# Rebuilding the opening and the last projected quarter of a fused attention, normalisation and expert kernel, and placing its tiles at round addresses

## The chip, the core and the metric

The kernel runs on one core of one Trainium2 chip. The metric is the device time of one execution in microseconds. Six engines matter in the text: TensorE with its weight loads (PE, PEld), VectorE (DVE), ScalarE (ACT), GpSimd (POOL) and SyncE (SP), which issues most DMAs. Each engine plays one list of instructions in order and waits on semaphores.

## What is computed

The reference has 4 sequences of 512 tokens of width 512. Each is projected to keys and values, a test-time recurrence runs over 32 mini-batches of 16 tokens for 16 heads of width 32, and its output is normalised, projected, added to the input and normalised again. Then 8 experts (two for each token) and one shared feed-forward work on the tokens, and a last normalisation follows.

```python
k, v = x @ Wk.T, x @ Wv.T                      # heads of width 32; rotary on k
def step(W, kv):                               # 32 of these, one after the other
    kc, vc = kv
    z = einsum('bhsd,bhde->bhse', kc, W)
    grad = einsum('bhsd,bhse->bhde', kc, (z - vc) * inv_n)
    return W - LR * grad, z
x = layernorm(x + (layernorm(z) * gamma + beta) @ Wo.T)
routed = sum over the two best experts of (silu(x Wg) * (x Wu)) Wd
x = layernorm(x + routed + shared(x))
```

## The kernel before

Every large product is done in three matmuls on float32r pieces: a tile is split into a high part (an ACT copy, for instance `xh`, `GH`, `XH`, `OH`) and a low part (a subtraction on DVE or POOL, `xl`, `GL`, `XL`, `OL`), and high times high, high times low and low times high are added up in one bank.

The 2048 tokens are worked on in four quarters of 512 (8 steps of the recurrence each). The first quarter's keys and values are projected ahead of the recurrence (`first`), behind `WARM` small matmuls that run while the first data are still on their way. Then the list `for n in range(LAST + 1)` builds 72 slots by hand. Slot n = 2s holds `scan_z` and `scan_r` of step s (PE, then a subtraction on DVE and four masked copies on ACT), slot 2s + 1 holds `scan_g` (PE) and the copies of the state W (ACT). Behind these, `slot(n)` places other work: the out-projection of a block of 128 tokens in `STAGES` (`t_one`, `t_wo_`, `t_three`, `router` on PE; `zt`, `stats_one`, `stats_two`, `norm_two`, `residual`, `out_rows` on the others), and half units of the projection of the next quarter (`products`, 6 matmuls of 512 columns; `HALVES` says how many in each of the 16 slots of a quarter). A quarter has 8 units of two halves: even units are keys (stationary `WH[:, 0]`, which shares its memory with the gate weights `GH[:, 0]`), odd ones values. `arrange` takes a unit out of its bank; a key passes through the rotary step over three slots (ACT, POOL, DVE shuffle, POOL, DVE add, DVE transpose), whose later parts wait in the list `later`.

In the opening, `wo_scale`, `wo_gamma`, `wo_sum`, `wo_bias`, `wo_means`, `wo_centre`, `wo_high` and `wo_low` make the out-projection's weights: its rows are scaled by gamma, the mean over rows is taken off, and the result is split into `OH` and `OL`. The first user is `t_wo_(0)` in slot 7.

From slot 48 on no quarter is left to project. There the generator `shared_01` hands out the shared expert in pieces: a quarter of a gate and up product (`gate_up_steps`, eight pieces of 6 matmuls for a weight block w and a token quarter q) or a quarter of a down product (`down_steps`). `FILL` gives each slot a budget; a piece costs 1.3. The tokens that these products read come from `turn_x(i)`: four transposes into a bank, then `XH` on ACT and `XL` on DVE; quarters 0 and 2 go to `XH0`, 1 and 3 to `XH1`. Bank 6 is also used by `t_one` and `router`, bank 7 by `t_wo_` and `t_three`; banks 4 and 5 by projections and by the first pieces of the shared expert. Behind slot 71 come the rest of the shared blocks 0 to 3, the routing, 23 expert strips (`gate_up_r` with 256 columns, `gate_up_s` with one strip of 128 tokens, `down_r`), the other shared blocks, and the sums.

Tiles are placed one behind the other in the order in which they are declared, small ones taking a multiple of 32 bytes. Added up, `xh`, `xl`, `GH`, `GL`, `ah`, `XH0` and `XL0` start at a multiple of 128 bytes, `XH1`, `XL1`, `RH`, `RL`, `OH`, `OL` and `oh`, `ol` 32 bytes behind one.

Of the kernel before, what the change touches and what calls it, by code (L numbers as in the profile page):

```python
# [12 lines left out]
NT = 16  # L13
# [9 lines left out]

HALVES = (2, 1, 2, 0, 2, 1, 1, 0, 2, 1, 1, 0, 2, 1, 0, 0)


WARM = 14
# [51 lines left out]
def program(nc, xT, xtok, wkT, wvT, woT, gam, bet, wg, wgu, wd, wsgu, wsd, cosd, sind, maskd, negid, identd, lowd, constd, upd, out):  # L79
    ctx = ExitStack()  # L80
    with ctx:
# [9 lines left out]

        x1 = sb(ctx, "x1", [NT, 512])
        ident = sb(ctx, "ident", [128])
# [8 lines left out]
        logits = sb(ctx, "logits", [NT, 8])  # L102
        comb = sb(ctx, "comb", [NT, 8])
        low = sb(ctx, "low", [8, 8])
        mhalf = sb(ctx, "mhalf", [1])
        st = sb(ctx, "st", [4, 6])
        mv = sb(ctx, "mv", [4, 2])
        rstd = sb(ctx, "rstd", [4, 2])
# [9 lines left out]
        eid = ctx.enter_context(nc.sbuf_tensor("eid", [128, RT], mybir.dt.int32))  # L118
# [64 lines left out]
        def split_g(w, ks=(0, 2)):  # L183
            p = w % 2
            f = (gused[w - 2],) if w >= 2 else (a_last[w],)
            out = gdone_.get(w, ())
            for k in ks:
                out += split(GH[:, p, k:k + 2, :], GL[:, p, k:k + 2, :], graw[:, rawp(w), k:k + 2, :], gloaded[w], free=f, rest=PO if w < 2 else DV)
            gdone_[w] = out
# [14 lines left out]
        def high_g0(k):  # L204
            return AC.op(lambda e: e.activation(GH[:, 0, k:k + 2, :], xr[:, k:k + 2, :], ACT.Copy), gloaded[0], a_last[0])

# [25 lines left out]
        mask = part(pa, "late", "mask", [64])  # L232
# [3 lines left out]
        W = [part(pa, "late", "WA", [256]), part(pa, "late", "WB", [256])]  # L236
        colsum = part(pa, "late", "colsum", [512])
        onesr = part(pa, "late", "onesr", [128], F32R)
# [3 lines left out]
        x1f = part(pa, "late", "x1f", [4, 128])  # L242
        wgs = part(pa, "late", "wgs", [4, 8])

# [27 lines left out]
        red = part(ctx, "first", "red", [3, NT])  # L272
        ce = sb(ctx, "ce", [4, 2, 8])
# [9 lines left out]

        ah = sb(ctx, "ah", [2, 2, 512], F32R)
# [76 lines left out]
        def wo_sum(key, src, tok, at):  # L361

            a = PO.op(lambda e: e.tensor_tensor(sums[:, at, :], src[:, 0, :], src[:, 1, :], ALU.add), tok[0], tok[1])
            b = PO.op(lambda e: e.tensor_tensor(sums[:, at + 1, :], src[:, 2, :], src[:, 3, :], ALU.add), tok[2], tok[3])
            t_sum[key] = PO.op(lambda e: e.tensor_tensor(sums[:, at, :], sums[:, at, :], sums[:, at + 1, :], ALU.add), a, b)
# [989 lines left out]
```

How the kernel before makes its waits and increments, by code:

```python
    def play(self, eng):  # L62
        for it in self.items:
            if it[0] == "w":
                eng.wait_ge(it[1], it[2])
            else:
                ins = it[1](eng)
                if it[2] is not None:
                    ins.then_inc(it[2], it[3])
```

## Time and profile before

| | us |
|---|---|
| median of 3 runs | 742.47 (741.02 to 742.95) |
| the profiled execution | 742.71 |
| its span, first to last instruction | 740.9 |
| PE busy in the span | 712.2 (96%) |
| DVE, ACT, POOL busy | 451.5, 343.7, 344.2 |

PE is the engine to look at: the chain of work that ended last lies on PE for 88% of the span. A busy PE still hides two kinds of time, matmuls that follow one another at a wider pitch, and stretches in which the clock that is granted to it is at the lower of its two levels. Pitch is read from the start times of neighbouring rows, the clock from the table of stretches.

### The profile page before, as it was taken

The numbers are of one execution on the slowest core, as the hardware profiler recorded it, in microseconds if no ns is written. First come the engines' busy times: TensorE is split into PE (matmuls) and PEld (weight loads), VectorE is DVE, ScalarE is ACT, GpSimd is POOL, SyncE is SP. The second block draws the span as 40 slices with busy tenths as digits, with TensorE's granted clock in tenths as the row PEclk, the third lists the DMA queues.
The fourth block names the chain that finished last, engine by engine and source line by source line (L and its number), as shares of the span: only waits on it lengthen the run. The fifth ranks groups of instructions, "written<-read, shape, count | busy, mean of one in ns | idle before, by whom it ended". The sixth has DMA issues, their size and how long they took to land.

```text
span 740.9 us, 17740 instructions
## 1 busy us (share of the span) xinstructions
PE 712.2 (96%) x7472; PEld 597.1 (81%) x7472; DVE 451.5 (61%) x753; ACT 343.7 (46%) x663; POOL 344.2 (46%) x361
## 2 busy tenths in 40 slices
PE   9997999999979998999999999999999999999994
PEld 8665788888867777778888898999989978888883
DVE  3755574575554455358883876676666627777554
ACT  5542454453444544242112576777767733241232
POOL 2784665566554644001102375565655335536332
PEclk9998999999999999999999999999999999999998
DMA  8120121112023213000402389999999875424221
GB/s 272 70 74 2 60 86 33 31 62 85 31 74 100 88 60 130 0 28 1 170 1 58 123 270 339 319 328 288 318 326 326 290 229 162 124 84 114 72 86 71
DMA packets 53263, 99.71 MB, mean 135 GB/s; under 512 B 5120, under 2 KB 14080, under 8 KB 53184
## 3 DMA queue, kind: packets, MB, share of 16 engines
q1 hardware_dynamic: 47504, 79.96, 32.0%
q0 software_dynamic: 5680, 18.62, 8.2%
q8 instruction: 59, 0.97, 0.5%
q14 instruction: 20, 0.16, 0.1%
HBM read 79.95 MB, written 18.61 MB: 133 GB/s over the span
## 4 chain that ended last, share of the span: by engine, by line
PE 88%; DVE 5%; ACT 2%; POOL 2%; DMA 1%; issue 1%; SPq 0%; POOLq 0%; DVEq 0%; ACTq 0%
PE bank L693 23%; PE bank L717 11%; PE bank L401 11%; PE bank L1120 11%; PE bank L608 7%; PE bank L1168 6%; PE bank L532 4%; PE bank L507 4%; PE bank L1137 3%; PE bank L1095 2%; PE bank L640 2%; DMA RAW<-in_wsgu 1%; PE bank L577 1%; PE bank L655 1%; PE bank L304 1%
## 5 line engine op out<-in xcount | busy, mean ns | idle before, releaser
L199 POOL TENSOR_TENSOR xl<-RAW,xh 128x1024 fp32r<-128x1024 f32 x31 | 75.1, 2422 | 122.6 <-ACT xh L198 95.1
L214 ACT ACTIVATE ah<-sg 128x512 fp32r<-128x512 f32 (+1 forms) x64 | 33.6, 525 | 158.4 <-DVE sg L669 149.2
L693 PE MATMUL bank<-XH,GH 128*128 128x512 f32 x256 | 103.1, 403 | 4.0 <-DVE XL L215 2.5
L693 PE MATMUL bank<-XL,GH 128*128 128x512 f32 x256 | 101.0, 395 | 0.0
L693 PE MATMUL bank<-XH,GL 128*128 128x512 f32 x256 | 101.0, 394 | 0.0
L215 DVE TENSOR_TENSOR GL<-RAW,GH 128x1024 fp32r<-128x1024 f32 (+2 forms) x63 | 81.1, 1325 | 10.8 <-ACT GH L214 9.7
L550 POOL TENSOR_SCALAR rstd<-mv 128x1 f32<-128x1 f32 x48 | 14.4, 300 | 142.9 <-DVE mv L549 142.2
L1056 POOL DMA_INDIRECT xg<-x1d,idxu x39 | 49.8, 1276 | 61.6 <-DVE idxu L1037 40.4
L518 DVE TENSOR_TENSOR r<-bank,vst 128x256 f32<-128x256 f32 x64 | 26.4, 422 | 84.0 <-PE bank L507 83.3
L1120 PE MATMUL bank<-RH,GH 128*128 128x256 f32 x256 | 72.9, 285 | 0.0
L1120 PE MATMUL bank<-RH,GL 128*128 128x256 f32 x256 | 71.5, 279 | 0.0
L1120 PE MATMUL bank<-RL,GH 128*128 128x256 f32 x256 | 71.5, 279 | 0.0
L214 ACT ACTIVATE GH<-RAW 128x1024 fp32r<-128x1024 f32 (+2 forms) x69 | 65.4, 996 | 1.8 <-DMA RAW<-in_wsgu 1.2
L669 DVE TENSOR_TENSOR sg<-sg,bank 128x512 f32<-128x512 f32 (+1 forms) x64 | 35.0, 547 | 51.2 <-PE bank L693 30.3
L521 ACT ACTIVATE r<-r,mask 128x128 f32<-128x128 f32 x128 | 41.0, 391 | 43.7 <-DVE r L518 43.7
L693 PEld LDWEIGHTS bank<-XH,GH 128*128 128x128 f32 x256 | 48.4, 189 | 15.5 <-ACT oh L582 2.2
L215 DVE TENSOR_TENSOR al<-sg,ah 128x512 fp32r<-128x512 f32 (+1 forms) x64 | 37.3, 583 | 37.8 <-ACT ah L214 37.1
L693 PEld LDWEIGHTS bank<-XH,GL 128*128 128x128 f32 x256 | 48.5, 189 | 11.2
L693 PEld LDWEIGHTS bank<-XL,GH 128*128 128x128 f32 x256 | 48.5, 190 | 10.2
L401 PE MATMUL bank<-xh,GH 128*128 128x512 f32 x128 | 53.4, 418 | 0.0
L401 PE MATMUL bank<-xl,GH 128*128 128x512 f32 x128 | 50.5, 394 | 1.4 <-POOL xl L747 1.4
L717 PE MATMUL bank<-xh,ah 128*128 128x512 f32 x128 | 51.0, 398 | 0.4 <-ACT sg L667 0.3
(218 smaller groups left out, 1765.5 us busy)
## 6 DMA issues: line engine op xcount, KB each, us to landing
RAW<-in_wgu SPq DMA_DIRECT2D x23, 1024.0 KB
RAW<-in_wd SPq DMA_DIRECT2D x23, 512.0 KB
yd<-RAW SPq DMA_DIRECT2D x39, 256.0 KB
RAW<-in_wsgu SPq DMA_DIRECT2D x14, 512.0 KB
x<-in_xtok SPq DMA_DIRECT2D x16, 256.0 KB, 3.8
x1d<-x SPq DMA_DIRECT2D x16, 256.0 KB, 2.1
RAW<-in_wsd SPq DMA_DIRECT2D x8, 512.0 KB
out_x<-x SPq DMA_DIRECT2D x16, 256.0 KB, 2.0
```

Of the source, the lines that this page charges most:

```text
L199: b = PO.op(lambda e: e.tensor_tensor(DL[:, p, :, :], draw[:, rawp(w), :, :], DH[:, p, :, :].bitcast(F32), ALU.subtract), a, dloaded[w], *f)
L214: a = AC.op(lambda e: e.activation(hi, src, ACT.Copy), *tokens, *free)
L215: b = rest.op(lambda e: e.tensor_tensor(lo, src, hi.bitcast(F32), ALU.subtract), a, *tokens, *free)
L401: t = PE.op(lambda e, k=k, wt=wt, xx=xx, n=n: e.matmul(bank[b][:], wt[:, j, k, hg * 128:hg * 128 + 128], xx[:, k, :], start=(k == 0 and n ...
L521: rtok[h] = AC.op(lambda e, b=b: e.activation(r4[:, :, b, :], r4[:, :, b, :], ACT.Copy, scale=mask[:, 32 * b:32 * b + 1]), s, t_c2)
L608: t = PE.op(lambda e, k=k, aa=aa, ww=ww, n=n: e.matmul(bank[b][:], aa[:, k, :], ww[:, k, :], start=(n == 1), stop=(n == 12)), state["oh"], ...
L669: m = DV.op(lambda e: e.tensor_tensor(sg[:, w, 0:cols], sg[:, w, 0:cols], bank[bu][:, 0:cols], ALU.mult), a, tu)
L693: t = PE.op(lambda e, b=b, k=k, c=c, wt=wt, xx=xx, n=n: e.matmul(bank[b][:], wt[:, p, k, c:c + 128], xx[h][:, k, :], start=(n == 1), stop= ...
L717: t = PE.op(lambda e, b=b, k=k, j=j, aa=aa, ww=ww, n=n: e.matmul(bank[b][:], aa[:, ap, k, j * 128:j * 128 + 128], ww[:, p, k, :], start=(n ...
L1056: PO.items.append(("i", lambda e, h=h: e.indirect_dma_start(xg[:, j % 2, h, :], None, x1d, bass.IndirectOffsetOnAxis(ap=idxu[:, first + h: ...
L1120: t = PE.op(lambda e, b=b, k=k, c=c, wt=wt, xx=xx, n=n: e.matmul(bank[b][:, 0:256], wt[:, pw, k, c:c + 128], xx[:, p, k, :], start=(n == 1 ...
L1168: t = PE.op(lambda e, b=b, k=k, h=h, aa=aa, ww=ww, n=n: e.matmul(bank[b][:], aa[:, p, k, h * 128:h * 128 + 128], ww[:, pw, k, :], start=(n ...
```

## The change

- Opening: 10 warm-up matmuls in place of 14. The transposes `a4` and `a6` of two key units leave the place ahead of the value units and go into `later`, so that they stand behind the first `scan_r`. Quarter 1's halves are handed out by a list of their own, `OPENING`. Of the four low parts of quarter 1's input, two stay on POOL and two go to DVE, by way of `later`; the three additions for the mean of the weights go from POOL to DVE, also by `later`. `wo_bias` moves from slot 1, bank 7, to slot 2, bank 6, behind `wo_means`.
- Last projected quarter: `UNITS` projects the key units 0, 2, 4 and 6 in places 0, 1, 2 and 4. The gate weights of the first shared block are split in slots 41 and 42 (before: 45 and 46), the turn-ins of tokens go to slots 44 (two), 45 and 46, in banks 6 and 7 (before: slots 46 and 47, banks 4 and 5), and the table load for Silu to slot 36 (before: 41).
- Shared expert: the budget begins in slot 47, `down_steps(1, 0)` is put ahead of `gate_up_steps(0, 1)`, and block 1's gate split goes to slots 51 and 52 with its low part on DVE (before: 52 and 53, POOL).
- Homes: declarations are put in another order with three fillers, so that every large tile starts at a multiple of 1024 bytes.

The diff, cut to its core:

```diff
+UNITS = (0, 2, 4, 1, 6, 3, 5, 7)
 HALVES = (2, 1, 2, 0, 2, 1, 1, 0, 2, 1, 1, 0, 2, 1, 0, 0)
-WARM = 14
+OPENING = (1, 1, 0, 1, 2, 1, 2, 0, 2, 1, 2, 0, 2, 1, 0, 0)
+WARM = 10
...
+        sb(ctx, "padh", [88])
         x1 = sb(ctx, "x1", [NT, 512])
...
+        part(pa, "late", "padl", [288])
...
+        sb(ctx, "padf", [136])
         ah = sb(ctx, "ah", [2, 2, 512], F32R)
...
+        def high_g1(k):
+            return AC.op(lambda e: e.activation(GH[:, 1, k:k + 2, :], graw[:, 0, k:k + 2, :], ACT.Copy), gloaded[1], a_last[1])
+
+        def low_g1(k, a):
+            b = DV.op(lambda e: e.tensor_tensor(GL[:, 1, k:k + 2, :], graw[:, 0, k:k + 2, :], GH[:, 1, k:k + 2, :].bitcast(F32), ALU.subtract),
+                      a, gloaded[1], a_last[1])
...
-        def wo_sum(key, src, tok, at):
+        def wo_sum(key, src, tok, at, Q):
...
-            t = PE.op(lambda e: e.matmul(bank[7][:], onesr[:].bitcast(F32), sums[:, 0, :], start=True, stop=True),
-                      t_ones, t_sum["bias"], *free[7])
+            t = PE.op(lambda e: e.matmul(bank[6][:], onesr[:].bitcast(F32), sums[:, 0, :], start=True, stop=True),
+                      t_ones, t_sum["bias"], *free[6])
...
         first(1, [3])
-        a4()
-        a6()
...
-            b = (PO if q == 1 else DV).op(lambda e: e.tensor_tensor(xl[:, k, :], xr[:, k, :], xh[:, k, :].bitcast(F32), ALU.subtract), a, tok, last_unit[0])
-            xs[q, k] = (a, b)
+            def rest():
+                b = (PO if q == 1 and k < 2 else DV).op(...)
+                xs[q, k] = (a, b)
+            if q == 1 and k >= 2:
+                later.append(rest)
+            else:
+                rest()
...
-            if n == 47:
-                turn_x(2)
-                turn_x(1)
+            if n == 44:
+                turn_x(0, base=6)
+                turn_x(1, base=6)
...
-            if n in (46, 47):
-                turn_x(3 * (n - 46))
-            if n == 41:
+            if n == 45:
+                turn_x(3, base=6)
+            if n == 46:
+                turn_x(2, base=6)
+            if n == 36:
                 AC.op(lambda e: e.activation(rstd[:, 3, 0:1], mhalf[:], ACT.Silu), t_mh)
             if q + 1 < NB:
-                for _ in range(HALVES[loc]):
+                for _ in range((HALVES if q else OPENING)[loc]):
...
-            if n == 1:
-                wo_bias()
             if n == 2:
                 wo_means()
+                wo_bias()
...
-            if n in (45, 46):
-                g0 = high_g0(2 * (n - 45))
-                later.append(lambda: low_g0(2 * (n - 45), g0))
+            if n in (41, 42):
+                g0 = high_g0(2 * (n - 41))
+                later.append(lambda: low_g0(2 * (n - 41), g0))
...
-            if n in (52, 53):
-                split_g(1, (2 * (n - 52),))
+            if n in (51, 52):
+                g1 = high_g1(2 * (n - 51))
+                later.append(lambda: low_g1(2 * (n - 51), g1))
...
             yield from down_steps(0, 0)
+            yield from down_steps(1, 0)
             yield from gate_up_steps(0, 1)
-            yield from down_steps(1, 0)
...
-        FILL = {n: SCAN[n % 4] for n in range(48, 64)}
+        FILL = {n: SCAN[n % 4] for n in range(47, 64)}
...
+        later.extend([a4, a6])
         for k in range(4):
             split_x(1, k, xraw[1])
-        wo_sum("bias", wob, t_wob, 0)
-        wo_sum("mean", wor, t_wosc, 2)
+        wo_sum("bias", wob, t_wob, 0, PO)
+        later.append(lambda: wo_sum("mean", wor, t_wosc, 2, DV))
```

## Rows read from the trace of the kernel before

**Rows 1.** The waits of PE: who waited for whom, us in total, times, longest

```profile
PE bank L608 <- DVE OL L387: 4.0, 1, 4.0
...
PE bank L693 <- DVE XL L215: 2.5, 2, 2.0
...
PE bank L693 <- ACT sg L667: 1.3, 1, 1.3
...
PE bank L608 <- DVE ol L587: 1.0, 1, 1.0
```

**Rows 2.** Table of stretches: length, PE busy (instructions), granted clock, DMA share, GB/s

```profile
62.00:68.60 6.60, 5.76 (x28) 0.50 0.01 2
...
294.00:297.30 3.30, 3.30 (x8) 0.50 0.31 119
435.00:585.00 150.00, 150.00 (x1033) 1.00 0.94 315
```

**Rows 3.** Timeline of PE, opening: start, length, line, tiles, count

```profile
1.45 6.14 PE L304 MATMUL bank<-colsum 128*128 128x128 f32 x28 [1.45 <-DVE colsum L300]
...
30.20 0.65 PE L507 MATMUL bank<-WA,RAW 32*32 32x64 f32 x32
...
44.98 1.02 PE L375 MATMUL bank<-RAW,onesr 128*128 128x512 f32 x2
...
68.22 0.85 PE L507 MATMUL bank<-WA,RAW 32*32 32x64 f32 x32
```

**Rows 4.** Timeline of PE in an undisturbed quarter: starts of slots 24 to 28

```profile
127.73 0.65 PE L507 MATMUL bank<-WA,RAW 32*32 32x64 f32 x32
...
131.70 1.10 PE L532 MATMUL bank<-r,RAW 32*32 32x64 f32 x64
...
134.69 0.65 PE L507 MATMUL bank<-WA,RAW 32*32 32x64 f32 x32
...
137.69 1.10 PE L532 MATMUL bank<-r,RAW 32*32 32x64 f32 x64
...
142.43 0.65 PE L507 MATMUL bank<-WA,RAW 32*32 32x64 f32 x32
```

**Rows 5.** Timeline of DVE in the opening

```profile
29.36 1.29 DVE L442 STREAM_TRANSPOSE RAW<-RAW 128x512 f32<-128x512 f32 x2
30.58 2.46 DVE L447 STREAM_TRANSPOSE vst<-bank 128x512 f32<-128x512 f32 x4
33.17 0.75 DVE L518 TENSOR_TENSOR r<-bank,vst 128x256 f32<-128x256 f32 x2
...
53.67 2.82 DVE L387 TENSOR_TENSOR OL<-x,OH 128x512 fp32r<-128x512 f32 x2
```

**Rows 6.** Timeline, PE and DVE, slots 44 to 47

```profile
202.45 0.87 DVE L518 TENSOR_TENSOR r<-bank,vst 128x256 f32<-128x256 f32 x2 [3.28 <-PE bank L507]
...
202.76 0.50 PE L401 MATMUL bank<-xh,GH 128*128 128x512 f32 x1
...
203.87 0.71 DVE L613 SCALAR_TENSOR_TENSOR x<-bank,rstd,x 128x512 f32<-128x512 f32 x1
...
209.72 0.66 PE L631 MATMUL bank<-ident,x 128*128 128x128 f32 x4
...
211.78 0.18 DVE L549 BATCH_NORM_AGGREGATE mv<-st 128x2 f32<-128x6 f32 x1
...
215.79 1.94 PE L655 MATMUL bank<-ident,x 128*128 128x128 f32 x8 [3.94 <-DVE XL L215]
```

**Rows 7.** Table of stretches for L693 alone: a product from XH0, one from XH1

```profile
659.50:670.75 11.25, 11.02 (x48) 9.01 (x48) 1.00 0.17 57
...
692.20:703.70 11.50, 11.33 (x48) 8.94 (x48) 1.00 0.06 23
```

**Rows 8.** Timeline of PE: third and last matmul of one 48 of L1120

```profile
486.64 0.28 PE L1120 MATMUL bank<-RH,GL 128*128 128x256 f32 x1
...
491.89 0.28 PE L1120 MATMUL bank<-RH,GL 128*128 128x256 f32 x1
```

More of the change, by code:

```diff
@@ L89, in program @@
         bank = [ctx.enter_context(nc.psum_tensor(f"bank{i}", [128, 512], F32)) for i in range(8)]
+        ident = sb(ctx, "ident", [128])
+        logits = sb(ctx, "logits", [NT, 8])
+        low = sb(ctx, "low", [8, 8])
+        st = sb(ctx, "st", [4, 6])
+        mhalf = sb(ctx, "mhalf", [1])
+        mv = sb(ctx, "mv", [4, 2])
+        rstd = sb(ctx, "rstd", [4, 2])
+        eid = ctx.enter_context(nc.sbuf_tensor("eid", [128, RT], mybir.dt.int32))
+        sb(ctx, "padh", [88])
         x1 = sb(ctx, "x1", [NT, 512])
-        ident = sb(ctx, "ident", [128])
         RAW = sb(ctx, "RAW", [2, 4096])
@@ L187, in split_g @@
             for k in ks:
-                out += split(GH[:, p, k:k + 2, :], GL[:, p, k:k + 2, :], graw[:, rawp(w), k:k + 2, :], gloaded[w], free=f, rest=PO if w < 2 else DV)
+                out += split(GH[:, p, k:k + 2, :], GL[:, p, k:k + 2, :], graw[:, rawp(w), k:k + 2, :], gloaded[w], free=f, rest=DV)
             gdone_[w] = out
@@ L242, in program @@
         x1f = part(pa, "late", "x1f", [4, 128])
+        W = [part(pa, "late", "WA", [256]), part(pa, "late", "WB", [256])]
+        onesr = part(pa, "late", "onesr", [128], F32R)
+        mask = part(pa, "late", "mask", [64])
         wgs = part(pa, "late", "wgs", [4, 8])
+        part(pa, "late", "padl", [288])
         vst0 = sb(pa, "vst0", [8, 256])
@@ L272, in program @@
         red = part(ctx, "first", "red", [3, NT])
+        comb = part(ctx, "first", "comb", [NT, 8])
         ce = sb(ctx, "ce", [4, 2, 8])
@@ L769, in slot @@
                     fn(i)
-            if n in (46, 47):
-                turn_x(3 * (n - 46))
-            if n == 41:
+            if n == 45:
[3 more added lines that the diff above has]
+            if n == 36:
                 AC.op(lambda e: e.activation(rstd[:, 3, 0:1], mhalf[:], ACT.Silu), t_mh)
             if q + 1 < NB:
-                for _ in range(HALVES[loc]):
+                for _ in range((HALVES if q else OPENING)[loc]):
                     halves[0] += 1
-                    u, second = divmod(halves[0] - 1, 2)
-                    u %= 8
-                    last_proj[0] = products(q + 1, u, 4 + u % 2, (2, 3) if second else (0, 1))
+                    at, second = divmod(halves[0] - 1, 2)
+                    at %= 8
+                    u = UNITS[at] if q == 2 else at
+                    last_proj[0] = products(q + 1, u, 4 + at % 2, (2, 3) if second else (0, 1))
                     if second:
                         a_last[u % 2] = last_proj[0]
-                        later.append(arrange(q + 1, u, 4 + u % 2, last_proj[0]))
+                        later.append(arrange(q + 1, u, 4 + at % 2, last_proj[0]))
             if loc >= 14 and q + 2 < NB:
```

26 lines of the change are left out of this document (9 added, 17 removed).

## The prediction, made before the changed kernel ran

> **What bounds the kernel now.** I read the waits of PE first, then the table of stretches with the granted clock, then the timelines of the places that these name. PE is busy for 96% of the span and on the chain that ended last for most of it, so only time that PE loses can be won. It loses it in three ways. First, waits: 4.0 us in slot 7, where the first out-projection waits for the low part of its weights; 3.94 us in slot 47, where a turn-in waits for the XL of the one before it; 2.0 and 0.5 us ahead of first gate products; 1.3 and 1.0 us behind short queues [rows 1, 6]. Secondly, behind the three long ones PE runs at the lower of its two levels (0.50 of 2.4 GHz) for a while: 6.6 us after the first, 3.3 us after the last [rows 2]. Thirdly, the pitch of the big matmuls differs with the operand: 48 of them that stream XH0 take 11.02 us, 48 that stream XH1 take 11.33 us, on the same line at the same clock [rows 7]. In the 150 us of expert strips PE is busy throughout [rows 2], so what is won before them should reach the end.
>
> **The change part by part.** All sums are made against the profiled execution's 742.71 us.
>
> (a) WARM. 28 records of warm-up take 6.14 us, 0.21 us each; four matmuls fewer are 8 records, 1.7 us [rows 3]. But they ran at the lower level, as their pitch tells (four transposes of 128 columns take 0.66 us, tail included, at the upper one [rows 6]), and real matmuls in their place would too until the clock rises. Ends: 0 and 1.7 us. I take the middle, 0.9: at half clock half of the freed time's work gets done.
>
> (b) The opening, slots 0 to 7. Before, PE goes from the first scan_z at 30.20 to that of slot 8 at 68.22, 38.0 us, and does 9 halves [rows 3]. After, I follow DVE, which is the late engine. Its last key add ends near 28.7 (0.75 earlier than before, from (a)). The two key transposes (1.29) are no longer ahead: value transposes 2.46, to 31.2; scan_r's two subtractions 0.75, to 31.9 (before 33.9); then the key transposes, to 33.2, which is when scan_g(0) can run; before, it stood behind 12 matmuls whose low parts POOL made one by one. Then the two xl that DVE now makes: two such subtractions beside a busy POOL took 2.82 us, 1.41 each, against 0.7 for a DVE operation by itself [rows 5, 6], so to 36.05. Three sums follow, one still beside POOL's sums: 1.4 + 0.7 + 0.7, to 38.85. Queued behind them are scan_r(1) and the first rotary step; who waits is wo_means on PE. PE does scan_z(0) at 29.3, one half to 33.2, scan_g(0) to 34.3, the second half as xl comes to 36.5 and scan_z(1) to 37.6, and idles 1.25 us. wo_means and wo_bias take 1.02 each [rows 3], so scan_g(1) starts at 40.9.
>
> From there undisturbed lengths hold [rows 4]: a slot with scan_z and two halves 3.97, one with scan_g, t_one and a half 2.99, one with scan_g, t_wo_ and router 4.74 (0.9 of it router). A half is 6 x 0.23 = 1.38. Slots 3 to 7: 2.5 + 3.97 + 2.99 + 3.97 + 3.84 = 17.3. Is OL ready at 55.5, when t_wo_(0) wants it? On DVE: wo_centre behind the rotary add to 44.9, scan_r(2), a block transpose, wo_centre to 47.6; the first wo_low pair to 49.5; the second stands behind scan_r(3), the block's statistics and a shuffle and ends between 55.7 and 56.5. So 0.6 us of wait, in place of 4.0, and no fall of the clock. Slot 8 starts at 40.9 + 17.3 + 0.6 = 58.8 (58.9 with the rounding of steps), with 8 halves done instead of 9, which costs 1.38 later: 68.22 - 58.9 - 1.38 = 7.9 us, of which (a) is 0.9. **(a) 0.9, (b) 7.0.** Ends of (b): 2 (below) and 9.
>
> On DVE the rows say that a two-input operation beside POOL costs about twice its 0.7 us [rows 5, 6]. The Trainium skill (SBUF — State Buffer, "SBUF: two separate sides") says why: a DVE operation with two SBUF inputs and a GpSimd one hold a shared port pair exclusively, and the later one blocks. By it each of the three sums could wait out a whole POOL operation, which speaks against giving them to DVE; that is the second rival's mechanism. The trace agrees, with 1.41 against 0.7 us.
>
> (c) Turn-ins, slots 44 to 47. Key units first make the rotary table's memory free by slot 42, so XH0 may be written in slot 44. The gate splits (two DVE subtractions, two ACT copies) go to slots 41 to 43, where DVE is idle for 3.28 us ahead of slot 44's scan_r [rows 6] and the two take some 2.5; I cost them at nothing, and if that cover were gone scan_r(44) would come later by what is over. What goes: 3.94 us of idling, and the lower clock behind it (eight transposes in 1.94 us instead of about 1.1 [rows 6], and three matmuls near twice their pitch): 0.8 + 0.5 us. What comes: bank 7 is freed for turn_x(1) by stats_two's DVE operation, which ends at 204.58, while PE would be there 0.5 us after 202.76: 1.3 us. Bank 6 is freed for turn_x(2) by bn_aggr, which ends at 211.96, while t_three ends at 210.2: 1.8 us [rows 6]. 5.2 - 3.1 = **2.1**. Queued behind these waits on PE are two halves and scan_g(47). Ends: 0.4, if the clock falls in the thin stretch of slot 46, and 5.2.
>
> (d) Slots 48 to 63. The XL wait of 0.5 and the Silu wait of 1.3 go [rows 1]. The new budget gives 2, 1, 1, 1 pieces in a group of four slots (2, 1, 2, 0 before); an act_part then falls just ahead of scan_r(50) on DVE and ahead of a second piece in slot 56. No row has that order; nearest are short waits of 0.2 to 0.3 us, ends 0 and 1.3. I take 0.2. **1.6.** Block 1's low gate parts leave POOL for DVE, two operations of the kind of (c) in slots 52 and 53, where DVE waits for PE as in slot 44: nothing, or at most a late scan_r. SP's issues and POOL's down split are not moved; the Silu table load only changes its slot on ACT, which is idle half of the time.
>
> (e) Slots 64 to 71. The turn-ins of quarter 1 are followed by three pieces of down(1, 0), which read nothing new: the 2.0 us wait and the lower clock (8 matmuls at 0.43 instead of 0.23 us: 1.6) go [rows 1, 2], also the 1.0 us for ol, as no act_part is ahead of stats_one(15). New: an act_part in slot 67 stands ahead of stats_two(15), whose result t_three(15) wants three pieces later. No row shows it; ends 0 and 3.9, and I take 1.7, near the queue waits of 1.0 to 2.0 us. **2.9.**
>
> (f) Homes. Of the lines with 512 columns, those whose streamed and stationary tiles start at the same distance from a multiple of 128 bytes run like XH0's; a product from XH1 has its streamed tile 32 bytes off its weights and takes 0.31 us more per 48 [rows 7]. Eight such products: 2.5 us. The strips' L1120 streams RH, 32 bytes off GH, too: 45 intervals in 5.25 us, 116.7 ns [rows 8], about half of XH1's 236. In XH0's proportion it would be 113.5: 768 x 3.2 = 2.5 us. Here DMA is busy 0.94 of the time [rows 2], so I take 2.0. **4.5**; ends 0 and 5.
>
> A rule speaks against (f). The rows show two pitches at one clock, 230 and 236 ns over whole products. The Trainium skill (TensorE: Matmul & The Clock Gate, "Wait — 56ns, not 53.3ns?") gives the warm distance as columns over 2.4 GHz plus 2.5 ns, with no place for an address. By it (f) is nought. The trace doesn't agree: both values lie over its 216.
>
> Sum: 0.9 + 7.0 + 2.1 + 1.6 + 2.9 + 4.5 = 19.0, so 723.7 in an execution like the profiled one, and **723.5** against the median, which lies 0.24 lower.
>
> **The rivals.**
> *Homes do nothing.* The two pitches come from something else about quarters 1 and 3. For it: no row tells how a home could slow a stream. Against it: one line, one weight tile, one clock, and only the streamed tile differs [rows 7]. 723.5 + 4.5 = 728.0.
> *The opening stays late.* Every DVE step beside POOL costs 1.4 to 1.8, OL comes 2.4 us later, t_wo_(0) waits 3.0 us and the clock falls again (2.6). (b) is 2: 728.5. For it: rows 5.
> *The tail's waits only change place.* (c) and (e) are nought: the clock falls in slot 46, and t_three(15) waits long. 728.5.
> *Slower: equal starts collide.* If tiles that start alike hinder each other, all 1578 fast matmuls of 512 columns pay. At XH1's price (6.5 ns) that is 10.3 us against the 14.5 won elsewhere; it decides from 9.2 ns. At twice the price, 13 ns, 742.5 - 14.5 + 20.5 = 748.5. Against it: L401 streams xh against weights that start alike, and is at the narrow pitch.
>
> **How the numbers follow.** Forecast (719 to 727) 0.53, homes 0.13, opening 0.17, tail 0.10, slower 0.02, several together and so within 0.3% 0.02, two together or better than 719 0.03. The range takes in the single rivals and the upper ends of (b) and (c): 715 to 731.5. A measurement tells about 0.3% from no change: faster 0.96, same 0.02, slower 0.02.
>
> **What would show it.** Slot 8's scan_z near 58.9 with a wait for OL under 1 us; no stretch at 0.50 between the warm-up and the end; new waits of L655 on DVE of 1 to 2 us in slots 44 and 46; XH1's 48 in 11.02; L1120 under 115 ns. Wrong it would be if OL is still awaited for 3 us, or if slot 46 runs at the lower level.

## The result and the profile after

| | before | after |
|---|---|---|
| median, us | 742.1 (4 runs, 741.02 to 742.95) | 731.51 (4 runs, 730.34 to 731.92) |
| ratio, 95% interval | | 0.9859 [0.9844, 0.9875] |
| profiled execution, us | 742.71 | 730.34 |
| its span, us | 740.9 | 728.5 |

The changed kernel is 10.6 us faster by the medians and 12.4 by the two profiled executions. 723.5 was forecast, with a range up to 731.5; the measured 731.51 lies just above its upper end. The three executions without a trace lie at 731.49 to 731.92.

The first view is the waits of PE in the changed kernel (who waited for whom, us in total, times, longest), which answers [rows 1].

```profile
PE bank L642 <- ACT x L631: 1.9, 1, 1.9
PE bank L728 <- DVE x L731: 1.8, 2, 1.0
...
PE bank L666 <- DVE mv L560: 1.4, 1, 1.4
PE bank L666 <- DVE x L624: 1.4, 1, 1.4
PE bank L543 <- ACT r L532: 0.9, 3, 0.4
...
PE bank L619 <- DVE OL L400: 0.4, 1, 0.4
```

The 4.0 us for OL are 0.4, the turn-in's 3.9 and the two for XL are gone. In their place stand three waits that were forecast, `t_three(15)` (L642, 1.9) and the two turn-ins (L666), and two that were not: down products (L728) that wait for DVE to empty a bank.

The second view cuts the span into stages. Its rows are from the timeline of PE (start, length, line, tiles) and give the starts of slots 0, 8, 44, 48 and 63, of the first routed product, and of the first and the last gate-up product of the late shared blocks.

```profile
29.68 0.43 PE L518 MATMUL bank<-WA,RAW 32*32 32x64 f32 x16 [0.34 <-DVE RAW L449]
...
59.31 0.41 PE L518 MATMUL bank<-WA,RAW 32*32 32x64 f32 x13
...
194.24 0.36 PE L518 MATMUL bank<-WA,RAW 32*32 32x64 f32 x11
...
214.02 0.37 PE L518 MATMUL bank<-WA,RAW 32*32 32x64 f32 x12
...
274.96 0.42 PE L543 MATMUL bank<-r,RAW 32*32 32x64 f32 x16
...
404.39 0.36 PE L1142 MATMUL bank<-RH,GH 128*128 128x256 f32 x1
...
587.11 0.39 PE L704 MATMUL bank<-XH,GH 128*128 128x512 f32 x1
...
695.91 0.39 PE L704 MATMUL bank<-XH,GH 128*128 128x512 f32 x1
```

The differences of such starts, made in the same way for other kernels of this study, are the lengths of the stages in us. "Work only" is the changed kernel with the addresses of before, "addresses only" the kernel before with the new ones, "mended" comes below.

| stage | before | addresses only | work only | after | mended |
|---|---|---|---|---|---|
| up to slot 0 | 30.20 | 29.18 | 29.34 | 29.68 | 28.80 |
| slots 0 to 7 | 38.02 | 37.74 | 29.54 | 29.63 | 30.08 |
| slots 8 to 43 | 133.52 | 133.57 | 134.73 | 134.93 | 134.95 |
| slots 44 to 47 | 20.57 | 21.73 | 19.83 | 19.78 | 16.70 |
| slots 48 to 62 | 62.99 | 63.08 | 60.81 | 60.94 | 60.94 |
| slot 63 to the first routed product | 132.39 | 131.47 | 130.31 | 129.43 | 126.58 |
| expert strips | 181.48 | 182.72 | 181.41 | 182.72 | 181.48 |
| late shared blocks, to the last gate-up | 109.88 | 108.80 | 109.88 | 108.80 | 108.80 |
| from there to the end | 31.86 | 31.51 | 32.08 | 32.60 | 31.50 |

Two entries are to be corrected before they are read as gains: the opening now does one half less, which comes back in slots 8 to 43 (1.41), and one piece of the shared expert (1.38) has moved from slots 48 to 62 into slots 44 to 47. The stages behind slot 63 show what the addresses do, since work only and before agree there but for the known waits: the expert strips are 1.2 to 1.3 longer with them, the late shared blocks 1.1 shorter.

The third view is the timeline of PE again, for the pitch: first and last matmul of a product of 48 with XH1 in the changed kernel, and the third and the last of a routed product, as in [rows 8].

```profile
630.63 0.39 PE L704 MATMUL bank<-XH,GH 128*128 128x512 f32 x1
...
641.29 0.39 PE L704 MATMUL bank<-XH,GL 128*128 128x512 f32 x1
...
497.35 0.28 PE L1142 MATMUL bank<-RH,GL 128*128 128x256 f32 x1
...
502.75 0.28 PE L1142 MATMUL bank<-RH,GL 128*128 128x256 f32 x1
```

47 intervals in 10.66 us are 226.8 ns, the pitch of XH0, as forecast. 45 intervals in 5.40 us are 120.0 ns where [rows 8] have 116.7: the routed products became slower, not faster. [rows 8] show one of the better ones: over all sixteen such products the mean is 117.2 before and 119.9 after.

### The profile page after: what moved, and what is told of

It reads as the page before. It is cut to its first block, busy times and chain, and to the rows that moved or that the text cites. A ratio compares the mean times of both kernels' runs of the same rounds, so it can differ in the third digit from the quotient of the medians.

```text
span 728.5 us, 17730 instructions
## 1 busy us (share of the span) xinstructions
PE 705.4 (97%) x7464; PEld 593.1 (81%) x7464; DVE 460.9 (63%) x760; ACT 343.0 (47%) x663; POOL 331.6 (46%) x354
## 4 chain that ended last, share of the span: by engine, by line
PE 67%; DVE 14%; POOL 5%; ACT 5%; issue 4%; DMA 3%; SPq 1%; POOLq 0%; DVEq 0%; ACTq 0%
PE bank L704 12%; PE bank L1142 11%; PE bank L414 8%; PE bank L1190 6%; PE bank L619 6%; PE bank L728 5%; PE bank L543 4%; PE bank L518 3%; PE bank L1159 3%; DVE x L731 2%; PE bank L1117 2%; POOL xg L1243 2%; DMA xg<-yd,SI 2%; DVE x L1251 2%; PE bank L651 2%
## 5 line engine op out<-in xcount | busy, mean ns | idle before, releaser
L225 DVE TENSOR_TENSOR GL<-RAW,GH 128x1024 fp32r<-128x1024 f32 (+2 forms) x63 | 83.2, 1359 | 10.0 <-ACT GH L224 8.8
L224 ACT ACTIVATE GH<-RAW 128x1024 fp32r<-128x1024 f32 (+2 forms) x67 | 63.3, 994 | 0.7 <-DMA RAW<-in_wgu 0.3
L728 PE MATMUL bank<-xh,ah 128*128 128x512 f32 x128 | 51.1, 399 | 2.0 <-DVE x L731 1.8
```

The source lines that it names most:

```text
L224: a = AC.op(lambda e: e.activation(hi, src, ACT.Copy), *tokens, *free)
L225: b = rest.op(lambda e: e.tensor_tensor(lo, src, hi.bitcast(F32), ALU.subtract), a, *tokens, *free)
L728: t = PE.op(lambda e, b=b, k=k, j=j, aa=aa, ww=ww, n=n: e.matmul(bank[b][:], aa[:, ap, k, j * 128:j * 128 + 128], ww[:, p, k, :], start=(n ...
```

## The experiments

**Does the sum of addresses come to 4.5 us?** `homes_only` is the kernel before with the new declarations alone, `work_only` the changed kernel without them.

```diff
+        sb(ctx, "padh", [88])
...
+        part(pa, "late", "padl", [288])
...
+        sb(ctx, "padf", [136])
```

> The kernel before with the new tile addresses alone, its order of work untouched. The forecast priced the addresses at 4.5 us (2.5 in the products of XH1, 2.0 in L1120), which gives 737.6. The trace of the changed kernel speaks for another sum: XH1's products there went from 233.4 to 226.7 ns each (2.5 us won), but the routed products of 256 columns went from 117.4 to 120.0 ns (about 2.0 us lost) and their companions of 512 columns from 232.4 to 227 (0.5 won), so 1.0 is left, 741.1; if the last stage is held by VectorE as the changed kernel's trace suggests, only 0.2 of it. If addresses do nothing, 742.1. Decisive in the trace: the pitch of L1120's successor, 120 if the address sets it, 117 if something in the new order does.

Measured: 741.56 against 741.32, ratio 0.9998 [0.9987, 1.0009]. The addresses alone give nothing that can be measured, although XH1's products have the narrow pitch in this trace too. In the table 0.9, 1.1 and 0.35 are won in the three stages with XH1's products and 1.2 are lost in the strips, which leaves 1.1. Another 1.1 are lost in slots 44 to 47, where the lower clock behind the old wait lasted 7 us instead of 3.5; no run shows that the addresses cause that.

> The changed kernel with the addresses of the kernel before: the opening and the last projected quarter alone. The forecast gives 742.5 less 14.5 (0.9 + 7.0 + 2.1 + 1.6 + 2.9), 728.0, and says that it loses 4.5 to the changed kernel. If the addresses are worth 1.0 or less, it stands within 1 us of the changed kernel, at 731 to 732.5. The routed products of 256 columns should then show 117.4 ns again and the late products of XH1 233.4.

Measured: 729.93 (729.73 to 732.31), ratio 0.9856 [0.9836, 0.9877], as fast as the changed kernel with its 0.9859. The two experiments agree: the new addresses as a whole are worth nothing that can be measured, and the 12.4 us are the work's.

**Which address costs?** `rh32` moves RH and RL alone by 32 bytes.

```diff
+        part(ctx, "first", "padr", [8])
         RH = part(ctx, "first", "RH", [2, 4, 256], F32R)
...
-        sb(ctx, "padf", [136])
+        sb(ctx, "padf", [128])
```

> The changed kernel with RH and RL alone put 32 bytes further on (their 32 bytes are taken from the padding behind them, so nothing else moves). If the address of the moving tile against that of the weights sets the pitch, the 256-column products go from 120.0 back to 117.4 ns, some 750 of them, 1.9 us won, and the products with RH as weights from 227 to 232.4, 77 of them, 0.4 lost: 1.5 faster than the changed kernel, 730.0. If the 120.0 comes from the new order of work (other engines reading at the same time), the pitch stays and the time too, 731.5.

Measured: 729.27 (728.11 to 732.87). The executions spread too widely to decide, but the strips take 181.54 instead of 182.72, and the routed products have 116.7 and 117.8 ns in turn, as before. The rows are the third and the last matmul of one of them in `rh32`, 45 intervals in 5.30 us.

```profile
496.37 0.28 PE L1143 MATMUL bank<-RH,GL 128*128 128x256 f32 x1
...
501.67 0.28 PE L1143 MATMUL bank<-RH,GL 128*128 128x256 f32 x1
```

So the address brings the pitch back, with the new order of work unchanged. `offsets` looks at other distances (the first filler shifts RH and RL along with XH1):

```diff
+        part(ctx, "first", "pad1", [16])
         XH1 = part(ctx, "first", "XH1", [4, 512], F32R)
...
+        sb(ctx, "pad0", [8])
         XH0 = sb(ctx, "XH0", [4, 512], F32R)
```

> A look at addresses: the changed kernel with XH0 and XL0 32 bytes off a multiple of 128, XH1, XL1, RH and RL 64 bytes off. If the moving tile's distance from the weights' tile sets the pitch, whatever tile it is, then XH0's 512-column products, 226.7 ns until now, show 233.4 at 32 bytes off; and at 64 bytes off the 512 columns show either 226.7 and the 256 columns 120.0 (64 is as good as 0) or 233.4 and 117.4 (64 is as 32). If it is the tile's place among its neighbours, XH0 stays at 226.7.

Measured: 735.68 in one execution, XH0's products at 233.4 ns and XH1's at 229.2 in all late products, the routed ones at 117.8 in fifteen of sixteen and at 113.3 in one. So it is not the tile but where it lies, and at 64 bytes the pitch lies between those at 0 and at 32. One question of the forecast's reasoning was left: a tile's own place, or its place against the weights? `w32_all` and `w32_only` shift the weights, on the mended version (below) with all tiles aligned; the second filler, in `w32_only` alone, puts the tiles behind the weights back on multiples of 128 bytes.

```diff
+        sb(ctx, "padg", [8])
         GH = sb(ctx, "GH", [2, 4, 512], F32R)
...
+        sb(ctx, "padx", [24])
         xh = sb(ctx, "xh", [4, 512], F32R)
```

> A look at addresses: the mended version, all tiles aligned, with the gate weights GH and GL and every large tile behind them 32 bytes further on, so that weights and moving tiles keep their distance. If the distance sets the pitch, XH0's and XH1's products stay at 226.7 ns and the routed ones of 256 columns at 120.0, 722 to 723.5. If the moving tile's own place does, they go to 233.4 and 117 to 118, some 5 us lost and 1.3 won.

> The same with the gate weights GH and GL alone 32 bytes off, all moving tiles on multiples of 128. If the distance sets the pitch, XH0's and XH1's products go to 233.4 ns and the routed ones to 117 to 118: 16 products of 48 lose 0.32 each, 5 us, and the routed products win 1.3 or so: 726 to 727. If the moving tile's own place does, nothing changes: 226.7, 120.0 and 723.

The rows are first and last matmul of a product of 48 in the timeline of PE, in w32_only and then in w32_all.

```profile
627.92 0.39 PE L706 MATMUL bank<-XH,GH 128*128 128x512 f32 x1
...
638.89 0.39 PE L706 MATMUL bank<-XH,GL 128*128 128x512 f32 x1
```

```profile
624.51 0.39 PE L705 MATMUL bank<-XH,GH 128*128 128x512 f32 x1
...
635.17 0.39 PE L705 MATMUL bank<-XH,GL 128*128 128x512 f32 x1
```

10.97 us are 233.4 ns, 10.66 us are 226.8. All eight late products of w32_only have 233.4, all eight of w32_all 226.7; the times are 728.33 and 723.12 in one execution each. The distance between the moving tile and the weights decides, as the forecast had it for 512 columns. For 256 columns w32_only has 120.0, not 117: there the moving tile lies 96 bytes behind the weights modulo 128, and that is no better than 0. Why a distance should matter is not shown by any run.

**Do the two halves of the work add up?** `opening_only` and `last_only` are the kernel before with one of them each, at the old addresses.

```diff
-WARM = 14
+OPENING = (1, 1, 0, 1, 2, 1, 2, 0, 2, 1, 2, 0, 2, 1, 0, 0)
+WARM = 10
...
+        later.extend([a4, a6])
...
+        later.append(lambda: wo_sum("mean", wor, t_wosc, 2, DV))
```

> The kernel before with the rebuilt first quarter alone (the second list of halves, ten warm-up products, the sums of the means on VectorE, the two late steps, the subtractions shared between GpSimd and VectorE, wo_bias a slot later), old addresses. The forecast gives 7.9 (0.9 for the warm-up, 7.0 for slots 0 to 7), so 734.2. The rival that the opening stays late gives 741.2. The changed kernel's trace puts slot 44 at 194.24 against 201.74, which is 7.5: 734.6.

Measured: 737.36 (735.26 to 738.12), 4.0 won instead of 7.5. Its trace shows slots 0 to 7 at 32.27 us, where work only has 29.54 with the same instructions in them.

```diff
+UNITS = (0, 2, 4, 1, 6, 3, 5, 7)
...
+            if n == 44:
+                turn_x(0, base=6)
+                turn_x(1, base=6)
...
+        FILL = {n: SCAN[n % 4] for n in range(47, 64)}
```

> The kernel before with the changes behind the opening alone: key blocks first in the last projected quarter, the four turn-ins in slots 44 to 46, the gate splits sooner, the pieces from slot 47, the new order of down and gate-up; old opening, old addresses. The forecast gives 2.1 + 1.6 + 2.9 = 6.6, so 734.7. What the changed kernel's trace shows instead is 2.2 + 0.7 + 2.2 = 5.1, so 736.2 against 741.3. If the parts don't add up and the opening's gain can only be had together with this one, it gives more: opening alone brought 4.0 and both together 11.4, so the rest would be 7.4, 733.9.

Measured: 736.35 (735.42 to 736.79), 5.0 won, and by stages 0.77 + 2.14 + 2.10 = 5.0. So this half is what the changed kernel's trace says. The two halves make 9.0 of the 11.4 that work only brings; the opening is what varies.

**Why does the opening end in two ways?** The same stretch of DVE and then of POOL, first in the changed kernel's profiled execution, then in that of `tail_keep`, whose opening has the same instructions.

```profile
33.98 3.40 DVE L760 TENSOR_TENSOR xl<-xr,xh 128x512 fp32r<-128x512 f32 x2
37.30 0.68 DVE L376 TENSOR_TENSOR RAW<-x 128x512 f32<-128x512 f32 x1
37.90 0.68 DVE L377 TENSOR_TENSOR RAW<-x 128x512 f32<-128x512 f32 x1
38.69 0.69 DVE L378 TENSOR_TENSOR RAW<-RAW 128x512 f32<-128x512 f32 x1
...
30.15 2.52 POOL L760 TENSOR_TENSOR xl<-xr,xh 128x512 fp32r<-128x512 f32 x2 [1.76 <-ACT xh L757]
...
33.88 1.26 POOL L377 TENSOR_TENSOR RAW<-RAW 128x512 f32<-128x512 f32 x1
35.28 1.54 POOL L378 TENSOR_TENSOR RAW<-RAW 128x512 f32<-128x512 f32 x1
38.88 1.63 POOL L441 TENSOR_TENSOR t<-kS,cosT 128x512 f32<-128x512 f32 x1 [2.05 <-ACT kS L432]
```

```profile
32.12 2.77 DVE L760 TENSOR_TENSOR xl<-xr,xh 128x512 fp32r<-128x512 f32 x2
34.81 1.78 DVE L376 TENSOR_TENSOR RAW<-x 128x512 f32<-128x512 f32 x1
36.52 1.75 DVE L377 TENSOR_TENSOR RAW<-x 128x512 f32<-128x512 f32 x1
38.37 1.56 DVE L378 TENSOR_TENSOR RAW<-RAW 128x512 f32<-128x512 f32 x1
...
30.14 2.53 POOL L760 TENSOR_TENSOR xl<-xr,xh 128x512 fp32r<-128x512 f32 x2 [3.61 <-ACT xh L757]
...
34.30 1.74 POOL L377 TENSOR_TENSOR RAW<-RAW 128x512 f32<-128x512 f32 x1
36.19 1.53 POOL L378 TENSOR_TENSOR RAW<-RAW 128x512 f32<-128x512 f32 x1
37.68 1.71 POOL L441 TENSOR_TENSOR t<-kS,cosT 128x512 f32<-128x512 f32 x1
```

In the first, the three sums come when POOL is through and take 0.68 each. In the second, DVE is earlier, each sum falls beside a sum or the rotary product (L441) of POOL, and both engines take longer. `wo_means` then waits on PE for the last sum, and the clock falls behind that wait (waits of PE and table of stretches of `tail_keep`, with the granted clock third from the end):

```profile
PE bank L388 <- DVE RAW L378: 2.9, 1, 2.9
```

```profile
42.00:44.00 2.00, 2.00 (x62) 1.61 (x64) 0.76 (x2) 1.05 (x3) 1.92 (x3) 0.50 0.04 8
```

That is the rival "the opening stays late" with the wait at another place. The Trainium skill (SBUF — State Buffer, "SBUF: two separate sides") has DVE and GpSimd hold a port pair exclusively for a whole instruction, the later one blocked; the trace agrees, with 1.78, 1.75 and 1.56 for sums that take 0.68 by themselves. Five traces end early (slots 0 to 7 in 29.5 to 29.7), five late: 32.1 to 32.5 where the clock falls to 0.50 between 41 and 45.5, 30.7 in `turns`, where it doesn't. In the early five POOL's second sum (L377 in the rows) takes 1.25 to 1.29 us, in the late five 1.72 to 1.80: there it is POOL that is held up by DVE's subtractions. In the early five POOL begins its low parts 1.74 to 1.81 us behind its previous operation, in the late five 1.88 to 3.61. What sets that gap, and so the order in which the two engines meet, was not found.

Two kernels try to break it. `bias_early` takes `wo_bias` out of the chain:

```diff
+            if n == 1:
+                wo_bias()
             if n == 2:
                 wo_means()
-                wo_bias()
```

> The changed kernel with wo_bias put back behind the products of slot 1, ahead of wo_means. In the changed kernel VectorE waits 1.46 in slot 2 for ScalarE's copy of the bias (the tile that the sums lie in must come free), and in the opening alone, where the two sums of the means took 1.76 each on VectorE beside GpSimd's sums instead of 0.68, that wait was 2.56 and slot 2 took 6.50 instead of 3.25. If the place of wo_bias carries the loss on, the wait is gone and the time falls by 0.5 to 2.5 in the executions that lose it, 729 to 731, with less spread. If VectorE's slow sums alone set it, the time stays at 731.5 and so does the spread.

Measured: 729.73 (729.34 to 731.74). The trace has an early opening of 29.71 us; slot 1 grew by 0.9 and slot 2 shrank by 1.2, so little is won where the ending is early, and a late ending was not traced. It does not decide.

```diff
-        wo_sum("bias", wob, t_wob, 0, PO)
         later.append(lambda: wo_sum("mean", wor, t_wosc, 2, DV))
+        later.append(lambda: wo_sum("bias", wob, t_wob, 0, DV))
```

> The changed kernel with all six sums of the weights of the output projection on VectorE, behind the two subtractions, and none on GpSimd. Seen so far: in the executions whose trace is known the opening ends in one of two ways, slot 8 at 59.0 to 59.3 or at 61.4 to 62.0; in the late ones VectorE's three sums take 1.78, 1.75 and 1.56 beside GpSimd's sums of 1.5 to 1.8, in the early ones 0.68 each, and TensorE waits 2.4 to 2.9 or 0.24 for them. If the two engines holding each other up is the cause, six sums of 0.68 (4.1) on VectorE alone end no later than three of 1.75 (5.3), the late ending is gone, and the times come close together at 729 to 730.5. If VectorE's length sets it, slot 8 comes 2 later in every execution, 732 to 733.

Measured: 729.26 (728.44 to 731.92). Slots 0 to 7 take 29.94 us, five of the six sums 0.69 and one 1.75. The rival, 2 us later in every execution, is out, but the spread of 3.5 us is not gone.

**What else varies, and what do the new waits cost?** `stats15` takes the last `stats_two` out of the queue behind a gate-up half.

```diff
-                if not pe:
+                if not pe and (fn is not stats_two or i < NT - 1):
                     fn(i)
...
+            if n == 4 * NT + 3:
+                stats_two(NT - 1)
```

> The changed kernel with the last tile's stats_two issued on VectorE in slot 67, right behind its t_wo_, and so ahead of the multiply of the gate_up half that slots 67 and 68 pull. In the changed kernel VectorE stands from 291.1 to 298.6 at the head of its queue for that half's products and does stats_two only at 300.6, 6 us after its product is there; t_three(15) then waits 1.9, and in two of the traces the clock falls to 0.50 for some 3.4 us behind that wait. Theory: the order on VectorE is the cause; the wait goes and 1.9 is won, 3.6 where the clock fell: 728 to 729.8. Rival: norm_two's chain over GpSimd is late anyway, the wait moves to the router or the next product and at most 0.5 is won, 731.

DVE in the changed kernel, then in `stats15` (in brackets the idle time before and who ended it):

```profile
298.62 0.69 DVE L680 TENSOR_TENSOR sg<-sg,bank 128x512 f32<-128x512 f32 x1 [7.56 <-PE bank L704]
300.00 0.69 DVE L225 TENSOR_TENSOR al<-sg,ah 128x512 fp32r<-128x512 f32 x1 [0.70 <-ACT ah L224]
300.61 0.75 DVE L624 SCALAR_TENSOR_TENSOR x<-bank,rstd,x 128x512 f32<-128x512 f32 x1
```

```profile
297.47 0.75 DVE L624 SCALAR_TENSOR_TENSOR x<-bank,rstd,x 128x512 f32<-128x512 f32 x1 [3.79 <-PE bank L619]
...
301.21 0.69 DVE L680 TENSOR_TENSOR sg<-sg,bank 128x512 f32<-128x512 f32 x1 [2.04 <-PE bank L704]
```

Measured: 728.09 (726.86 to 730.32). In the changed kernel DVE stands 7.56 us at the head of its queue for a product while the one that `stats_two` wants is long there; in `stats15` the order is turned and the wait of `t_three` is gone, the stage from slot 63 on 2.1 shorter (127.33 against 129.43). The profiled execution, 730.32, is the slowest of the four; its opening is late, with slots 0 to 7 at 32.52 us.

`turns` moves two turn-ins.

```diff
-                turn_x(1, base=6)
...
-                turn_x(2, base=6)
+                turn_x(2)
...
+            if n == 44:
+                turn_x(1, base=6)
```

> The changed kernel with turn_x(1) behind the products of slot 44 instead of ahead of them, and turn_x(2) in bank 4 instead of bank 6. In the changed kernel the one waits 1.38 for bank 7 behind stats_two and the other 1.39 for bank 6 behind the statistics of slot 46. Theory: both waits go and nothing comes late in their place, 2.8 won: 728.7. Rival: the splits that follow come later and the first gate-up piece in slot 47 waits for XL instead: half or nothing is won, 730 to 731.5.

Measured: 729.26 (727.80 to 730.53); slots 44 to 47 take 16.67 us instead of 19.78, so 3.1 are won there, and no wait takes their place. In this trace the clock falls behind the wait of `t_three`, which the changed kernel's own does not show (table of stretches, `turns`):

```profile
301.90:305.10 3.20, 3.20 (x10) 2.56 (x9) 0.08 (x1) 1.08 (x2) 0.00 (x0) 0.50 0.24 87
```

3.2 us at half the clock cost 1.6. `tail_keep` and `offsets` have the same fall at 307.5 and 308; six other traces with this wait (1.8 to 1.9 us) have none.

**What holds the final stretch?** `tail_keep` lets ACT take the next activation ahead of the last scaling.

```diff
-                    scale_pending()
+                    scale_pending(keep=1)
```

> The changed kernel with ScalarE's last scaling of a finished tile (L1265) held back by one more step in the final stretch, so that the activation of the next gate_up half doesn't queue behind a scaling that waits for GpSimd. In the changed kernel VectorE's multiply of the last gate_up comes 3.9 us behind the end of its products (1.1 in the kernel before), and TensorE then waits 0.85 for a bank. If that queue holds the final stretch, the lag falls below 2, the wait goes and 0.8 to 1.2 is won: 730.5. If the lag comes from the gathered rows and VectorE's joins before, the lag stays at 3 or more and nothing is won: 731.5.

DVE's multiply behind the last gate-up, in the changed kernel and in `tail_keep`; the last matmul of its products starts at 706.57 and at 710.28.

```profile
710.42 0.69 DVE L680 TENSOR_TENSOR sg<-sg,bank 128x512 f32<-128x512 f32 x1 [1.89 <-ACT sg L678]
```

```profile
710.78 0.69 DVE L680 TENSOR_TENSOR sg<-sg,bank 128x512 f32<-128x512 f32 x1 [1.74 <-PE bank L704]
```

The lag is 3.9 us in the one and 0.5 in the other, where DVE waits for the product itself, and the time from the last gate-up to the end falls from 32.60 to 31.50. The queue on ACT was the cause of the lag. What that is worth varies: `rh32`, `bias_early`, `sums_dve`, `stats15` and `turns`, with the changed kernel's order, have a lag of 2.9 to 3.3 us and take 31.62 to 32.10 for this stretch, so the gain is 1.1 against the changed kernel's profiled execution and 0.1 to 0.6 against these. The median is 732.12 (728.79 to 733.48). The profiled execution, 732.94, has the late opening (32.14) and the fall of the clock behind `t_three`. The others have no trace; the mean granted clock is 0.990 to 0.995 in those above 731 and 0.997 in the fastest.

**All together.** `mended` is the changed kernel with `sums_dve`, `stats15`, `turns`, `tail_keep` and `rh32`, and with the turn-ins of quarter 1 in two slots:

```diff
-                for i in range(4, 8):
-                    turn_x(i, base=i // 2 % 2 * 2)
+                turn_x(4, base=0)
+                turn_x(5, base=0)
...
+            if n == 65:
+                turn_x(6, base=2)
+                turn_x(7, base=2)
```

> The changed kernel with all of it together: the six sums on VectorE, stats_two(15) early, turn_x(1) and turn_x(2) moved, turn_x(6) and turn_x(7) a slot later than turn_x(4) and turn_x(5), the scaling in the final stretch held back, RH and RL 32 bytes off. If the parts add up: 1.9 (t_three's wait), 2.8 (turn-ins), 1.0 (the wait behind turn_x(4) to turn_x(7)), 1.1 (final stretch), 1.5 (addresses), on the best execution's 730.3: 722.0, and with the late opening and the fallen clock gone the executions should lie within 1.5 us of each other. If the freed time is taken back by the next waits as in the changed kernel, half of it: 726.

Measured: 721.63 (721.48 to 722.32), ratio to before 0.9736 [0.9719, 0.9754]. It beats both kernels, and its five executions lie within 0.9 us. Its longest waits of PE:

```profile
PE bank L318 <- DVE colsum L314: 1.5, 1, 1.5
PE bank L382 <- DVE RAW L379: 1.4, 1, 1.4
PE bank L1197 <- ACT RAW L1202: 1.1, 1, 1.1
```

None of the changed kernel's new waits of 1 us or more is left: the first is the start of the program, the second is `wo_bias` behind the six sums, the third stood in the kernel before too. On this quiet base the small terms can be measured.

```diff
-WARM = 10
+WARM = 14
```

> The mended version with 14 warm-up products instead of 10. The forecast prices the four at 0.9 with ends at 0 and 1.7: 722.5. In the changed kernel the third matmul of the first product starts at 6.74 against 7.89, 1.15 earlier, but the first scan_z only at 29.68 against 30.20, so 0.5 may be all that reaches the loop: 722.1.

Measured: 721.86 (721.12 to 722.15), 0.2 more, within the spread. In its trace the 28 records of warm-up take 5.21 us where [rows 3] have 6.14, and the third matmul of the first product starts at 6.96 against 6.49 in mended: four warm-up matmuls cost 0.5 there, not 1.15.

> The mended version with the tile addresses of the kernel before. VectorE lags TensorE by 0.5 us in its final stretch instead of 3 to 4, so nothing there should take a gain of TensorE back. If XH1's 6.7 ns per matmul are real time, eight products lose 2.5 us against the mended version, whose RH and RL have the old distance anyway: 724.1. The forecast says the same for XH1. If they are taken back elsewhere, as homes alone suggest (0.2 the wrong way), it stays at 721.6 to 722.3.

Measured, with the declarations of the kernel before: 723.75 (723.05 to 724.43), 2.1 more than mended.

> The mended version with RH and RL back on multiples of 128 bytes, as in the changed kernel. The forecast has aligned tiles 2.0 faster: 719.6. The traces have 120.0 ns instead of 117.8 to 118.9 for some 750 products and 227 instead of 235 for 77: 1.5 to 1.9 lost and 0.4 won, so 722.7 to 723.1. If the transfers of the expert strips hide it, 721.6.

Measured, without `padr`: 723.14 (722.13 to 723.54), 1.5 more. So both prices of an address are real time, one for and one against the change, and the final stretch no longer takes the first back.

> The mended version with the sums as in the changed kernel, those of the bias on GpSimd. If the two engines holding each other up cause the two endings of the opening, executions lie at 721.6 or 1.1 to 2.6 above, in two groups; if the spread came from the wait of t_three and its clock alone, which is gone here, all lie at 721.5 to 722.5.

Measured, with the sums as in the changed kernel: 721.75 (721.66 to 721.83), all five within 0.2 us and an early opening of 29.62 us in the trace. So it is not shown that the move of the sums cured the spread: on this base the late ending did not come up at all.

## Why the prediction was wrong, point by point

The profiled executions differ by 12.4 where 19.0 was forecast. By the table: 0.5 up to slot 0, 38.02 - 29.63 - 1.41 = 7.0 in the opening, 0.79 + 1.38 = 2.2 in slots 44 to 47, 2.05 - 1.38 = 0.7 in slots 48 to 62, and 2.1 from slot 63 to the first routed product (work only against before, where no address plays in). That is all of it: from slot 63 on the new addresses win 0.9 and 1.1 and lose 1.2, and the final stretch loses 0.7.

**(f) The addresses are the step that failed:** 4.5 forecast, nothing measured, 4.5 of the 6.6 that are missing. Its first half, XH1, was right: 2.5 forecast, 226.8 ns measured, 2.3 by stages and 2.1 in `m_homes_old`. Its second half had the wrong sign. The forecast carried a proportion from 512 to 256 columns and made 116.7 ns into 113.5; measured are 120.0, and `m_aligned` (by the medians) and `rh32` (by the strips) put 1.5 and 1.2 us on it, after the 0.4 that the 84 matmuls of L1159 win. On the quiet base all aligned against the old addresses is 0.6 (723.14 against 723.75), so by the medians the whole change of addresses is worth between nothing and 0.6. Among [rows 7, 8] there was no row of a 256-column product with its tile aligned, so the bound should have reached below nothing there. The ends 0 and 5 left the loss out because the text took the address for a cost in one direction. In the profiled execution part of the first half was also taken back by the final stretch, 32.60 against 32.08; other traces with XH1 aligned have 31.5 to 32.1 there.

**(a) The warm-up** was mis-sized: 0.9 forecast, 0.2 in `m_warm14`. The third matmul of the first product does start 1.15 earlier (6.74 instead of 7.89), but little of that reaches the loop: slot 0 starts anywhere between 28.6 and 29.7 among traces with 10 warm-up matmuls.

**(b) The opening** was right in the profiled execution: slot 8 at 59.31 for 58.9, the wait for OL 0.4 for 0.6, no lower clock, 7.0 for 7.0. Part of that is luck: the two subtractions of DVE take 3.4 us where 2.8 were forecast, the three sums 2.1 where 2.8 were. What the forecast had as one value was two: its step "1.4 + 0.7 + 0.7" for the sums is 0.68 three times in the early ending, and in the late one two or three of them take 1.56 to 1.78. The late ending costs 1.1, with the fall of the clock 2.5 to 2.9. The forecast put this as a rival with a chance of 0.17, for OL; it comes at `wo_means` instead.

**(c) The turn-ins** were right: 2.2 for 2.1, waits of 1.38 and 1.39 for 1.3 and 1.8, no lower clock.

**(d) Slots 48 to 62** were mis-sized: 0.7 for 1.6. The new order's waits are 0.4, 0.3 and 0.3 where 0.2 in all was taken, and slots 50, 54, 56 and 61 are longer by 0.4 to 0.6 each than slots of the new order with the same work (58, 52 and 53).

**(e) From slot 63 on** 2.1 for 2.9. `t_three(15)` waits 1.9 for the 1.7 forecast. The text said that the down pieces behind the turn-ins read nothing new; that is so, but they wait for a bank that DVE empties behind its four subtractions for XL (2.46 us), 1.0 us.

**The median** lies 1.2 above the profiled execution. Its other executions have no trace; what the traces of kernels with the same code at those places show as ways to lose that much are the late opening and the fall of the clock behind `t_three` (1.6). The mean granted clock of the other three is lower, 0.992 to 0.995 against 0.997, but which of the two it was stays open. **The range** took the rivals one at a time: homes alone gave 728.0. On the 723.7 of the sum, homes at nothing (4.5), 2.1 less from (a), (d) and (e), and 1.2 of spread come together to 731.5.

**The rival "equal starts collide"** had its mechanism right for one line only: aligned starts do cost the 256-column products 2 to 3 ns, and nothing the 512-column ones. "Homes do nothing" was the right rival in its sum and wrong in its reason, and "the tail's waits only change place" held for 1.0 us of (e).

## What to carry to other kernels

A correction found at one shape is a number for that shape: before it is carried to another, a row of that other shape in the target state is needed, or a bound on both sides of nothing. Two engines that hold each other up don't have one duration but two arrangements, and a schedule that runs them side by side should be priced at both. Where an engine that is off the chain stands for 7 us at the head of its queue, what is queued behind it is worth a look: turning the order of two instructions won 2 us here, and in the final stretch up to 1.1.

## What the runs showed of the hardware

The pitch of these float32r matmuls at the upper clock depends on the distance, modulo 128 bytes, between the moving tile and the weights, and differently by length. 512 columns (late products): 226.7 ns at 0 (changed kernel), 233.4 at 32 (kernel before, `offsets`), 229.2 at 64 (`offsets`), 233.4 at 96 (`w32_only`). 256 columns: 119.7 or 120.0 at 0 (changed kernel), 116.7 or 117.8 at 32 (kernel before, `rh32`), 117.8 at 64 (`offsets`, one product of sixteen at 113.3), 120.0 at 96 (`w32_only`). Shifting both tiles alike changes nothing (`w32_all`). The two values at 32 and the one product at 113.3 say that for 256 columns the distance is not all. The Trainium skill (TensorE: Matmul & The Clock Gate, "Wait — 56ns, not 53.3ns?") has columns over 2.4 GHz plus 2.5 ns, by which an estimate is 215.8 and 109.2; the traces agree with neither value, and no run here shows a pitch as narrow.

A wait of 1.8 us or more on PE was followed by a stretch at 0.50 in some traces and not in others with the same code at that place. Behind the 1.8 to 1.9 us of `t_three` the clock fell in three traces of nine (`turns`, `tail_keep`, `offsets`) and not in the changed kernel's. Behind the 2.4 to 2.9 us of `wo_means` it fell in four of five, and not in `turns`.
